# Cross-attention on one core: context pieces of 17 products, the loads of q on ScalarE's queue, and another place for the scores of head 1

## The reference

```python
query = hidden_states @ Wq
keyt = enc @ Wk            # enc: the first 718 rows
valt = enc @ Wv
hs = _mha(query, keyt, valt)
ca_q1 = jnp.einsum('btc,th->bch', ca, Wq_ca)[:, indices, :]
ca_hs1 = _mha(ca_q1, residual, residual)
ca_hs2 = _mha(ca_hs1 @ Wq, ca @ Wk_ca, ca @ Wv_ca)
out = (hs + ca_hs2) @ Wout + b_out + residual
```

## Time and profile before

| | us |
|---|---|
| median of 3 runs | 1001.76 |
| lowest, highest | 997.12, 1004.11 |
| the profiled execution | 1004.24 |
| its span, first to last instruction | 1002.5 |

### The profile page before, as it was taken

How to read it: one execution, slowest core, us unless ns; L and a number is a source line. 1 busy time by engine, 2 the same in 40 slices (tenths; PEclk the granted TensorE clock), 3 DMA queues, 4 the chain that set the end, 5 groups by cost and what they waited for, 6 DMA issues and landing times.

```text
span 1002.5 us, 20727 instructions
## 1 busy us (share of the span) xinstructions
PE 985.5 (98%) x6740; PEld 964.2 (96%) x6740; DVE 652.0 (65%) x1129; ACT 490.8 (49%) x895; POOL 342.9 (34%) x286
## 2 busy tenths in 40 slices
PE   9989999999999999999999999999999999998998
PEld 8989889999999999999999999999999999997997
DVE  6544676667667766667676767676766666667444
ACT  7524555555554546464636364636464545446110
POOL 5212253434252516161515243333333333416000
PEclk9979999999999999999999999999999999999999
DMA  7959978797879797979797979788887878795354
GB/s 264 307 192 257 266 190 210 166 202 168 191 172 195 171 187 177 187 181 185 181 182 185 181 184 181 191 171 202 170 201 162 210 162 193 171 213 152 98 181 146
DMA packets 154169, 190.12 MB, mean 190 GB/s; under 512 B 80928, under 2 KB 108192, under 8 KB 154144
## 3 DMA queue, kind: packets, MB, share of 16 engines
q1 hardware_dynamic: 147456, 177.44, 75.6%
q10 hardware_dynamic: 6688, 12.35, 3.7%
HBM read 81.56 MB, written 19.95 MB: 101 GB/s over the span
## 4 chain that ended last, share of the span: by engine, by line
PE 85%; DVE 5%; SPq 4%; DMA 3%; ACT 2%; issue 1%; ACTq 0%; DVEq 0%
PE psS L744 21%; PE psB L779 20%; PE psB L784 10%; PE psS L719 7%; PE psT L760 6%; PE psS L888 6%; PE psT L806 4%; PE psT L812 2%; SPq L382 2%; DMA encT_raw<-in_encT_dram 1%; PE psB L861 1%; SPq L379 1%; PE psB L838 1%; PE psT L813 1%; PE psS L944 1%
## 5 line engine op out<-in xcount | busy, mean ns | idle before, releaser
L744 PE MATMUL psS<-encT_keep,Wk_keep 128*128 128x360 f32 x1440 | 253.7, 329 | 0.0
L744 PEld LDWEIGHTS psS<-encT_keep,Wk_keep 128*128 128x128 f32 x1440 | 237.3, 188 | 0.9 <-issue 0.2
L779 PE MATMUL psB<-PT_h,encN_h 120*128 120x400 f32 x576 | 202.3, 351 | 0.0
L779 PE MATMUL psB<-PT_l,encN_h 120*128 120x400 f32 x576 | 198.8, 345 | 0.0
L1130 ACT ACTIVATE probs<-psS,negmax 100x718 f32<-100x718 f32 x128 | 110.2, 861 | 129.2 <-DVE negmax L1522 129.0
L606 POOL TENSOR_TENSOR encT_keep<-encT_raw,encT_keep 128x718 fp32r<-128x718 f32 x45 | 79.7, 1771 | 181.6 <-ACT encT_keep L1159 179.3
L1546 DVE TENSOR_TENSOR kT<-psS,kT 128x718 fp32r<-128x718 f32 x80 | 72.4, 905 | 94.9 <-ACT kT L1154 94.7
L614 POOL TENSOR_TENSOR encN_l<-enc_raw,encN_h 120x768 fp32r<-120x768 f32 x48 | 92.6, 1930 | 91.4 <-ACT encN_h L1166 90.0
L597 POOL TENSOR_TENSOR Mbd<-Mbd,fmask 128x320 fp32r<-128x320 f32 x48 | 45.8, 954 | 226.7 <-DMA Mbd<-m_split 224.1
L784 PE MATMUL psB<-PT_h,encN_l 120*128 120x400 f32 x576 | 120.4, 344 | 0.7 <-POOL encN_l L614 0.7
L1154 ACT ACTIVATE kT<-psS 128x718 fp32r<-128x718 f32 x80 | 61.7, 771 | 115.2 <-PE psS L744 110.0
(11 more groups left out here) (245 smaller groups left out, 1643.5 us busy)
## 6 DMA issues: line engine op xcount, KB each, us to landing
kstack<-kT SPq DMA_DIRECT2D x64, 448.8 KB
kstack<-kT SPq DMA_DIRECT2D x192, 112.2 KB
enc_raw<-in_encN_dram SPq DMA_DIRECT2D x48, 360.0 KB, 5.6
encT_raw<-in_encT_dram SPq DMA_DIRECT2D x45, 359.0 KB, 6.4
kstack<-kT SPq DMA_DIRECT2D x32, 359.0 KB
kstack<-kT SPq DMA_DIRECT2D x32, 269.2 KB
kstack<-kT SPq DMA_DIRECT2D x32, 179.5 KB, 3.6
kstack<-kT SPq DMA_DIRECT2D x64, 89.8 KB, 3.5
```

Source lines behind the costliest of these rows:

```text
L744: mm = pe.matmul(keys_in(f, first)[:, half, 0:HALF], w[:, c, f * 128:(f + 1) * 128], e[:, c, k0:k0 + HALF], start=(j == 0), stop=(j == 3 * ...
L779: pe.matmul(psB[:, 1, 0:RH], eN[0][:, k, cc], PT[p][:, k, rows], start=(k == 0 and p == 0), stop=False)
```

## The change

Keys lie in chunks of 128 now: five full ones (640 keys) and a tail of 78. A piece has 15 products over the five full chunks. For the tail there are two in place of three: one takes 117 rows, of which 78 are high x high and 39 low (context) x high (P) for the first half of the tail; the other takes 78 rows of high x low and 39 of low x high for the second half. For that,

- `norm` writes the first 39 tail probabilities a second time behind the 718 (a further tensor_scalar on VectorE, with a wait before the main one), so that the transposes, now of 128 columns, bring them to rows 78 to 116;
- GpSimd makes the tail's low part first and in place (`tail_low`), then chunk 4, then the other two thirds: four instructions for three; `load_enc` and `enc_high` take chunks 4 and 5 first;
- ScalarE copies the tail's high part a second time (`enc_twice`);
- DMAs put the halves into place: two per batch in `tail_enc` and one in `tail_pt0` on SyncE's queue, behind load_x, and one in `tail_pt1` on ScalarE's queue at the end of the batch. context(i, 0) waits for `entail`, and pieces 0 and 3 wait for `pttail`, before the last two products.

`load_q(i + 1)` goes from SyncE's queue to ScalarE's, between pt_high(i, 4) and expo(i, 7), with its wait. scores(i, 1), its `rowmax` and its `expo` go from the end of the batch before to behind context(i - 1, 2), ahead of keys(i, 3); on VectorE norm(i, 1) goes behind k_low(i, 3). In stage 1 the load of heads 6 and 7 is issued ahead of that of the first context, and `enc0_high` and `enc0_low` go from behind q(1, 2) to behind q(1, 4). In the last batch GpSimd splits two blocks of Wout ahead of the context, not three.

```diff
-KP = (KEYS + KT - 1) // KT
+KP = 128
 KPAD = KT * KP
-HALF = KPAD // 2
+HALF = 360
+FULLK = KEYS // KP
+TAIL = KEYS - FULLK * KP
+TH = TAIL // 2
+TSTK = TAIL + TH
...
+        tail_low = enc_raw[0:KP, FULLK * C:KT * C].bitcast(F32R)
...
+        def third(c):
+
+            return slice(4, 6) if c == 0 else slice(2 * (c - 1), 2 * c)
...
+        def load_q(eng, b):
+            for p in range(2):
+                q3 = q_d[p].rearrange("(h d) n -> d h n", d=D)[:, :, bass.ds(b * S, S)]
+                eng.dma_start(raw(qst[p][0:D, :, :]), raw(q3)).then_inc(s["qin"], 16)
+                qh = q_d[0].rearrange("(h d) n -> d h n", d=D)[p * EX:(p + 1) * EX, :, bass.ds(b * S, S)]
+                eng.dma_start(raw(qst[p][D:STK, :, :]), raw(qh)).then_inc(s["qin"], 16)
...
-                    free("encN", PARTS * (b - 1) + c + 1, first)
-                    ks = slice(c * KQ, (c + 1) * KQ)
+                    free("encN", LOWS * (b - 1) + c + 2, first)
+                    if c == 0:
+                        free("entail", 32 * b, first)
+                    ks = third(c)
...
+                def tail_pt0(b):
+
+                    wait_apart(sp, s["ptlo"], HEADS * b + 4, s["passed_sp"])
+                    sp.dma_start(raw(PT[1][TAIL:TSTK, FULLK, 0:RH]), raw(PT[0][TH:TAIL, FULLK, 0:RH]))\
+                      .then_inc(s["pttail"], 16)
+
+                def tail_enc(b):
+
+                    wait_apart(sp, s["encN"], LOWS * b + 1, s["passed_sp"])
+                    for p in range(2):
+                        sp.dma_start(raw(eN[p][TAIL:TSTK, FULLK, :]), raw(tail_low[p * TH:(p + 1) * TH, :]))\
+                          .then_inc(s["entail"], 16)
...
+                sp.wait_ge(s["hlo"], 6)
+                load_heads(6, 2)
                 sp.wait_ge(s["wlo"], 5)
                 sp.dma_start(enc0_raw, encT[0].rearrange("(c p) k -> p c k", p=128)).then_inc(s["encin"], 16)
-                sp.wait_ge(s["hlo"], 6)
-                load_heads(6, 2)
                 sp.wait_ge(s["v2st"], 32)
-                load_q(0, first=True)
+                load_q(sp, 0)
...
-                        load_q(i + 1)
-                    else:
+                    tail_pt0(i)
+                    tail_enc(i)
+                    if not first:
...
-                        if not first:
-                            load_q(i + 1)
...
-                    for c in range(PARTS):
-                        ks = slice(c * KQ, (c + 1) * KQ)
-                        pool.wait_ge(s["encNhi"], PARTS * b + c + 1)
+                    pool.wait_ge(s["encNhi"], LOWS * b + 2)
+                    nc.gpsimd.tensor_tensor(tail_low, rawN[:, FULLK, :], eN[0][:, FULLK, :],
+                                            ALU.subtract).then_inc(s["encN"], 1)
+                    pool.wait_ge(s["encN"], LOWS * b + 1)
+                    nc.gpsimd.tensor_tensor(eN[1][:, FULLK - 1, :], rawN[:, FULLK - 1, :], eN[0][:, FULLK - 1, :],
+                                            ALU.subtract).then_inc(s["encN"], 1)
+                    pool.wait_ge(s["encN"], LOWS * b + 2)
+                    for c in range(1, PARTS):
+                        ks = third(c)
+                        pool.wait_ge(s["encNhi"], LOWS * b + c + 2)
                         nc.gpsimd.tensor_tensor(eN[1][:, ks, :], rawN[:, ks, :], eN[0][:, ks, :],
                                                 ALU.subtract).then_inc(s["encN"], 1)
-                        pool.wait_ge(s["encN"], PARTS * b + c + 1)
+                        pool.wait_ge(s["encN"], LOWS * b + c + 2)
...
-                for c in range(3):
+                for c in range(2):
                     wo_low(c)
                 enc_low(B - 1)
-                for c in range(3, FT):
+                for c in range(2, FT):
...
-                    for k in range(KT):
+                    for k in range(FULLK):
                         for p in range(2):
                             pe.matmul(psB[:, 1, 0:RH], eN[0][:, k, cc], PT[p][:, k, rows],
                                       start=(k == 0 and p == 0), stop=False)
-                    for k in range(KT):
-                        if u == 0 and k % KQ == 0:
-                            pe.wait_ge(s["encN"], PARTS * i + k // KQ + 1)
-                        mm = pe.matmul(psB[:, 1, 0:RH], eN[1][:, k, cc], PT[0][:, k, rows],
-                                       start=False, stop=(k == KT - 1))
-                    mm.then_inc(s["u"], 1)
+                    for n, k in enumerate((4, 0, 1, 2, 3)):
+                        if u == 0 and n in (0, 1, 3):
+                            pe.wait_ge(s["encN"], LOWS * i + (n + 1) // 2 + 2)
+                        pe.matmul(psB[:, 1, 0:RH], eN[1][:, k, cc], PT[0][:, k, rows], start=False, stop=False)
+                    if u == 0:
+                        pe.wait_ge(s["entail"], 32 * i + 32)
+                    if c == 0:
+                        pe.wait_ge(s["pttail"], 32 * i + 16 * half + 16)
+                    pe.matmul(psB[:, 1, 0:RH], eN[0][0:TSTK, FULLK, cc], PT[0][0:TSTK, FULLK, rows],
+                              start=False, stop=False)
+                    pe.matmul(psB[:, 1, 0:RH], eN[1][0:TSTK, FULLK, cc], PT[1][0:TSTK, FULLK, rows],
+                              start=False, stop=True).then_inc(s["u"], 1)
...
+                        scores(i, 1)
                     keys(i, 3)
                     if not first:
                         values(i - 1, 0)
...
                         context(i, 1)
                         scores(i + 1, 0)
                         b2_scores(i + 1, 1)
-                        scores(i + 1, 1)
...
+                def enc_twice(b):
+
+                    nc.scalar.activation(eN[1][0:TAIL, FULLK, :], rawN[0:TAIL, FULLK, :], ACT.Copy)\
+                      .then_inc(s["encNhi"], 1)
+
+                def tail_pt1(b):
+
+                    act.wait_ge(s["ptlo"], HEADS * b + HEADS)
+                    act.dma_start(raw(PT[1][TAIL:TSTK, FULLK, RH:R]), raw(PT[0][TH:TAIL, FULLK, RH:R]))\
+                      .then_inc(s["pttail"], 16)
...
                     else:
                         u_high(i - 1, 2)
+                        expo(i, 1)
                     k_high(i, 3)
...
                         enc_high(i, 0)
+                        enc_twice(i)
...
                     pt_high(i, 4, first)
+                    if not last:
+                        act.wait_ge(s["scores"], HEADS * (i + 1))
+                        load_q(act, i + 1)
                     expo(i, 7)
...
                         k_high(i + 1, 2)
                     pt_high(i, 7)
-                    if not last:
+                    if last:
+                        tail_pt1(i)
+                    else:
                         u_high(i, 1)
+                        tail_pt1(i)
                         expo(i + 1, 0)
                         b2_exp(i + 1)
-                        expo(i + 1, 1)
 
...
                 q_high(1, 2)
-                for c in range(CT):
-                    enc0_high(c)
                 head_high(6)
                 q_high(1, 3)
                 head_high(7)
                 q_high(1, 4)
+                for c in range(CT):
+                    enc0_high(c)
                 q_high(1, FT)
...
-                    dve.wait_ge(s["inv"], HEADS * i + h + 1)
+                    dve.wait_ge(s["inv"], 2 * (HEADS * i + h) + 1)
+                    nc.vector.tensor_scalar(P[h % PRING][0:S, KEYS:KEYS + TH],
+                                            P[h % PRING][0:S, FULLK * KP:FULLK * KP + TH], inv[:, h:h + 1],
+                                            None, ALU.mult).then_inc(s["inv"], 1)
+                    dve.wait_ge(s["inv"], 2 * (HEADS * i + h) + 2)
                     nc.vector.tensor_scalar(P[h % PRING][0:S, 0:KEYS], P[h % PRING][0:S, 0:KEYS], inv[:, h:h + 1],
                                             None, ALU.mult).then_inc(s["norm"], 1)
...
                     if not first:
                         u_low(i - 1, 2)
+                        rowmax(i, 1)
+                    k_low(i, 3)
                     norm(i, 1)
-                    k_low(i, 3)
                     if first:
```

More of the change, by code:

```diff
@@ L109, in program @@
         NP = FT + 1
+        LOWS = PARTS + 1
         HALFCOLS = slice(GT, 2 * GT)
@@ L327, in free @@
                         wait_apart(sp, s[name], n, s["passed_sp"])
-                def load_q(b, first=False):
-                    free("scores", HEADS * b, first)
-                    for p in range(2):
-                        q3 = q_d[p].rearrange("(h d) n -> d h n", d=D)[:, :, bass.ds(b * S, S)]
-                        sp.dma_start(raw(qst[p][0:D, :, :]), raw(q3)).then_inc(s["qin"], 16)
-                        qh = q_d[0].rearrange("(h d) n -> d h n", d=D)[p * EX:(p + 1) * EX, :, bass.ds(b * S, S)]
-                        sp.dma_start(raw(qst[p][D:STK, :, :]), raw(qh)).then_inc(s["qin"], 16)
                 def load_encT(b, c, first=False):
@@ L1805, in _ @@
```

(4 more changed lines are left out.)

10 lines of the change are left out of this document (5 added, 5 removed).

## The result

| | before | changed |
|---|---|---|
| median, us | 999.57 (4 runs) | 1033.61 (4 runs) |
| lowest, highest | 997.12, 1004.11 | 1030.29, 1037.03 |
| span of the profiled execution | 1002.5 | 1032.0 |

A forecast was written before the change was run, and what follows sets the result against it. TensorE, busy 98% of the span, was taken as the bound. Terms -17.6 + 2.0 + 7.5 - 8.2 + 1.5 + 1.3 = -13.5 us, from the median 1001.76 to 988.3; forecast's own range 983 to 994, overall 979 to 1007.

The forecast's parts named there:

- the first part of 6: q's four loads issued on ScalarE's queue, in time its wait for VectorE's maximum leaves: cost 0.
- Tail copies: SyncE's tail DMAs each batch land by about 546.5, before their products at 551: covered, no cost.
- Term 1: Context pieces on TensorE: one product of 18 goes, 96 times 0.183 us, -17.6 us.
- Term 2: Transposes in `turn` load 128 columns instead of 120: at most +2.8 us, nothing if hidden, +2.0 taken.
- Term 4: Head 1's scores moved behind the third context product: TensorE waits 0.5 us at each of 15 batch borders, +7.5 us.
- Term 5: Stage 1, weights of heads 6 and 7 ahead of the first context: TensorE idle and half clock go, -8.2 us.
- rival B: Stage 1's idle only moves, so its reordering gives 0 to -2 us: 995 to 997 us, chance 0.15.
- Term 3: VectorE's extra 39-column scaling in each `norm`: 0.2 us, 128 times, 26 us of an engine with idle time; by itself 0.
- rival A: VectorE's scaling at head 3 loses to GpSimd; TensorE's piece 5 waits 1.2 us per batch: around 1006 us, chance 0.22.
- The small terms of 6: Low part of head 5 late for turn(i, 6), +1.5 us; last batch's `enc_low` thirds later, +1.3 us.
- signs to watch: What traces should show for each claim, including batches of about 51.3 us; wrong if outside 51.0 to 51.6.

The follow-up runs named there:

- run 5: Kernel before with only q's four loads moved to ScalarE's queue, behind pt_high(i, 4): 1012.99 us against 1001.15, ratio 1.013.
- run 1: Changed kernel with q's loads back on SyncE's queue, behind lift(i + 1, 0): 1002.23 us against 1000.77 for the kernel before, ratio 0.9987.
- Run 7: Changed kernel with q's loads on SyncE's queue but ahead of lift(i + 1, 0): 1042.24 us against 1001.15 for the kernel before, ratio 1.0408.
- run 11: Kernel before with only q's loads moved to ScalarE's queue, behind pt_high(i, 5): 1007.32 us against 1002.44, ratio 1.0041.
- run 3: Changed kernel with q back on SyncE behind lift(i + 1, 0) and head 1's scores back in the batch before: 1005.98 us, ratio 1.0024 to the kernel before.
- run 10: As run 3, without the four tail copies and their waits, result incomplete: 992.89 us against 1001.20 for the kernel before, ratio 0.9915.
- run 12: As run 3, with v2's three loads issued by ScalarE behind pt_high(i, 4): 997.50 us against 1002.44 for the kernel before, ratio 0.9959.
- run 4: Kernel before with only stage 1's new order of loads and splits: 999.51 us, ratio 0.9978.
- run 6: Kernel before with only head 1's scores, maximum and exponential moved behind the third context product: 1007.45 us against 1001.15, ratio 1.0068.

## Why the prediction was wrong

**The step that failed is the first part of 6, q on ScalarE's queue, "Cost 0".** It priced the issue on the issuing engine and stopped there. q's loads had stood behind lift(i + 1, 0) in SyncE's queue; moved, they run beside it or ahead of it. The only sentence on lifts in that part, "SyncE's lift(i + 1, 1) waits for keys anyway, so nothing is gained", looked at the lift behind q and not at the one ahead of it. What stands behind a lift's landing was not asked: k_high(i + 1, 2). Measured: +12 us alone (run 5), 31 to 35 inside the changed kernel (run 1). Run 7 shows that q ahead of the lifts costs this on one queue as well, run 11 that with nearly the old order on the new queue k_high has its wait for kstack no more and only ScalarE's held time remains, some 5 us. That part, too, had been costed at 0.

The Trainium skill (DMA: Bandwidth & Descriptors, Issuing engines are not separate DMA queues) says that transfers started by different engines run on the same 16 DMA engines and interleave, and that a second issuing engine saves only its issue time. The traces agree: beside q the last lift took 6.8 us from its issue to k_high's start (median), with q behind it 4.3 or less (run 1). By this rule the step has a price, and the prediction did not draw on it.

**Tail copies, "Covered": wrong, +11 to +13 us (runs 3 and 10).** The prediction checked that the copies land in time for their product, and they do. It took the waits of load_v2 and lift for later than the copies, and so missed 2.3 us of issue, where SyncE had 1.5 us idle ahead of the first lift (547.22 to 548.71 before): in run 12, with as much taken out of it again, 6.5 to 8.5 of it come back.

**Term 1, right in size, not in effect.** Added over four batches, the distances between starts of the context products are 19.95 us a batch before and 18.91 in run 10: -1.04, where 6 x 0.183 = 1.10 was predicted. A product of 128 rows costs what one of 120 did, 0.185 us in the mean of each. Of the whole, though, run 10 has -0.51 a batch: TensorE had nearly every releaser in time at 51.9 and meets some that are not at 51.0, VectorE's UT above all. **Term 2:** the transposes take 3.88 us a batch before and 3.89 in run 10, so nothing, the lower bound and not the +2.0 taken. The weight load itself grew as the earlier trace rows says:

```profile
L792 PEld LDWEIGHTS psT<-ident,probs 100*128 100x128 f32 x768 | 79.2, 141 | 10.2 <-DVE P L1656 3.1 <-issue 2.8
```

**Term 4, right**: +6.3 to 6.8 us alone against +7.5, some 0.5 us at the context product. In the changed kernel about half of it is left: the context product starts 0.48 us behind the b2 product (572.78 to 573.26), just as u_low ends at 573.20.

**Term 5, right in place, wrong in worth.** The idle at 52 us and the half clock behind it are gone, as the windows above show against the earlier trace rows, and twelve products take 1.51 us again:

```profile
53.35 1.51 PE L1035 MATMUL psS<-kstack 80*128 80x64 f32 x12
...
61.27 3.12 PE L776 MATMUL psS<-encT_keep,Wk_keep 128*128 128x360 f32 x18
```

keys(0, 0) starts 7.99 us earlier; -8.2 was the term. But alone it is worth 1.3 us by the medians and 2.2 by the ratio (run 4, whose interval includes a ratio of 1). That is rival B's figure, 0 to -2, and nearly its mechanism: the idle only moves, though to after 75 us and not to the head's load. The term took one microsecond as given back; it was nearly all, half of it by the end of batch 0 and half behind the last mark.

**Term 3 and rival A.** The small scaling takes 0.24 us uncontended, 0.30 in the mean, and the big one grew from a mean of 648 ns to 831 (groups by line; then GpSimd and VectorE at head 6):

```profile
L1590 DVE TENSOR_SCALAR probs<-probs,inv 100x718 f32<-100x718 f32 x128 | 106.4, 831 | 4.5
...
L1586 DVE TENSOR_SCALAR probs<-probs,inv 100x39 f32<-100x39 f32 x128 | 37.9, 296 | 4.5
```
```profile
552.12 1.85 POOL L646 TENSOR_TENSOR encN_l<-enc_raw,encN_h 128x768 fp32r<-128x768 f32 x1 [1.94 <-ACT encN_h L1204]
...
552.30 2.06 DVE L1590 TENSOR_SCALAR probs<-probs,inv 100x718 f32<-100x718 f32 x1
```

The collision that rival A described exists, but at head 6, where the scaling starts 0.18 us behind GpSimd and ends 0.39 behind it; at head 3 VectorE won. It ends at 554.36, and the next operation, k_low, waits for k_high until 554.44 anyway, so it costs nothing where rival A had 1.2 us. The Trainium skill (SBUF — State Buffer, Who interferes with whom) has whoever issues first hold the shared pair for the whole instruction; the 2.06 us agree.

**The small terms of 6.** Neither shows: TensorE has no wait for the low part of head 5 in the changed kernel or run 10 (+1.5 was taken), and its wait for `enc_low` in the last batch is 0.5 us in both, where it was 0.7 (+1.3 was taken).

**The rivals and signs.** No rival had a transfer that comes late. The signs to watch did include "no TensorE wait on DMA, no ScalarE delay before u_high(i, 0)", and neither line would have shown this one: the wait is ScalarE's, at k_high. The sign that did show is the batch period: 54.07 us where 51.0 to 51.6 was required.

Still open: what lengthens the end of the span. In the runs without the new order of stage 1 (5, 6 and 11) the time after the last mark is within 0.3 us of before; in all runs with it, and in the changed kernel, it is 1.8 to 7.7 us longer, P1T's wait being the largest part in run 4. How q's 31 to 35 us divide between lateness and the low clock has only the estimate above, 24 us of waits and 13 of clock, and why the clock falls behind some borders and not behind others is open.

## What to carry to other kernels

When an issue moves to another queue, write down what it stood behind in the old one: it now runs beside that, and the time at which those transfers land, and the instruction that overwrites their source, must have slack for it. Small copies that are "in time" for their reader can still delay whatever is queued behind their issue. And a kernel at 98% of one engine may give back only part of the work taken from it: waits that were just covered come out when it gets 2% faster, here half (0.5 of 1.0 us a batch).

## What the runs showed of the hardware

Four loads that SyncE issues in 1.9 us took ScalarE 2.1 us in the changed kernel and 2.9 to 3.0 in runs 11 and 5 (medians), and in run 5 its following instruction stood with "issue" as its releaser until they were out. Beside q's packets, an issue of a lift that took 0.66 us in the kernel before took 1.30, a pair that took 2.02 took 2.56, and the last landed 6.72 us after its issue began. TensorE's clock fell to 1.2 GHz behind eight of 14 batch borders with an idle of 0.8 us behind the four products of the scores and up to 1.83 ahead of them. The longer idle ahead did not decide: the clock fell behind 0.38 and 0.81 us, and not behind 1.55 and 0.82.
